# Moving a reduction to the end of VectorE's slot in a software-pipelined attention and FFN kernel

## The chip, the cores and the metric

The kernel runs on one core of a Trainium2 chip. The metric is the device time of one execution, in microseconds (us); the time before is the median of three executions. The core's engines are TensorE (PE in the profile), VectorE (DVE), ScalarE (ACT), GpSimd (POOL) and SyncE (SP), which here issues all DMAs. Each engine works through its own list of instructions in the order in which the program wrote them; the lists meet only at semaphores.

## The reference

For 4 sequences of 1024 rows and 256 channels, and a context of 154 rows of 192 channels for each, the reference computes cross attention and a gated FFN whose inputs and weights are rounded to blocks of 4-bit floats:

```
x  = x + attention(layernorm(x), ctx)       # 16 heads of 64, softmax over the 154 context rows, then Wo, bo
xq = fp4(layernorm(x))                      # blocks of 16: largest |x| / 6 is the scale, 8 magnitudes
h  = silu(xq @ fp4(w_gate).T) * (xq @ fp4(w_up).T)      # 704 wide
x  = x + fp4(h) @ fp4(w_down).T
```

## The kernel before

The 4096 rows are 32 tiles of 128 rows. `schedule` runs one **step** for each tile (`t = 2 * pair + par`), and each engine has its own function `step` with the same shape: a loop over 8 **slots** `k`. A slot is the unit of the software pipeline: in slot `k` of step `t` the kernel works on the pair of heads `u = k` (a *unit*) of tile `t`, and on later stages of older units and tiles: `e = t-1` (the end of its attention, then its layernorm and rounding), `f = t-2` (gate and up products, in quarters), `d = t-3` (the rounding of the hidden values and the down product), `c = t-4` (the output). The flags `own`, `before`, `gate`, `down` and `out_` say which of these exist. The first steps and one group of four steps in every eight also prepare keys, values and projected values of a sequence (`setup`, the jobs).

One unit passes through these stages:

- PE slot `k`: `scores` writes the scores of unit `k` into one of two PSUM banks `ps_s` (three matmuls, high and low parts of fp32 values). It waits for the exponentials of unit `k-2`, which free the bank.
- DVE slot `k`: the largest score of each of the two heads, negated, into `negmax` (L884).
- ACT slot `k`: two exponentials `probs <- ps_s` with `negmax` as the bias, which also make the sums (L678). They wait for `max_v`, the semaphore of L884.
- DVE slot `k+1`: `invert_sums` makes `rsum` (L848). POOL slot `k+1`: `normalise` multiplies the exponentials by it (L511).
- PE slot `k+2`: `turn_probs` transposes them into the one bank `ps_t` (L1213). It waits until the low parts of the unit before it are out of that bank.
- ACT slot `k+3`: `weights_hi` copies `ps_t` into `pT_hi` (L572), the first work of the slot. DVE slot `k+3`: `weights_lo` takes the difference, `pT_lo` (L737, a helper that makes all low parts).
- PE slot `k+4`: `attend` multiplies by the projected values.

In the kernel before DVE's slot `k` is in this order: `invert_sums` of unit `k-1`; the low parts of unit `k-3` (and in slot 2 those of `xqT`, in slots 5 and 6 those of `hqT`); **the largest score of unit `k`**; then everything else: the output sum in slot 0, the low part of a query product (`q_lo`), the jobs, `stats` in slot 4, `silu` and `hidden` of one FFN quarter in slots 3 to 6, block maxima and scales, the powers that round the values, and the residual sum `x1` in slot 3.

ACT's slot `k` is: `weights_hi` of unit `k-3`, other high parts, `tanh` of a quarter in slots 3 to 6, the exponentials of unit `k`, and behind them in slot 2 the copy `y <- x1` (L698), in slot 4 the next tile's layernorm (`layer_norm1_out`, L601), in slot 5 the layernorm of `x1` into `xn` (L689). DVE's slot 5 reads `xn` (`largest(xn, ...)`, L764); POOL's slot 6 multiplies it by `xri` (L552) behind `normalise` of unit 5, and DVE's slot 6 waits for that before `power(xn, ...)` (L784).

Of the kernel before, what the change touches and what calls it, by code (L numbers as in the profile page):

```python
# [5 lines left out]
ALU = mybir.AluOpType  # L6
ACT = mybir.ActivationFunctionType
AX_X = mybir.AxisListType.X
# [15 lines left out]
def xattn_ffn_kernel(nc: bass.Bass, x, ctx_768, Wq, Wk, Wv, Wo, bo, w_gate, w_up, w_down, out):  # L24
# [8 lines left out]
    PAIRS = H // 2  # L33
# [7 lines left out]
    UM = 2 * M  # L41
# [13 lines left out]
    with ExitStack() as stack:  # L55
        def sb(name, shape, dt=F32):
            return stack.enter_context(nc.sbuf_tensor(name, shape, dt))

        def sem(name):
            return stack.enter_context(nc.semaphore(name))  # L60
# [29 lines left out]
        negmax = sb("negmax", [P, H])  # L90
# [5 lines left out]
        st2, mv2, rs2, nm2 = ln[1]  # L96
# [3 lines left out]
        x1 = [x1_both[:, i, :] for i in range(2)]  # L100
        y_xn = sb("y_xn", [P, 3 * C])
        y, xn = [y_xn[:, i * C:(i + 1) * C] for i in range(2)], y_xn[:, 2 * C:3 * C]
# [29 lines left out]
        def bank(name):  # L132
            return stack.enter_context(nc.psum_tensor(name, [P, 512], F32))

        ps_t, ps_q, ps_o, ps_m = (bank(n) for n in ("ps_t", "ps_q", "ps_o", "ps_m"))
        ps_s = [bank("ps_s0"), bank("ps_s1")]
# [26 lines left out]
        s_mm, max_v, exp_a, rsum_v, norm_p = (sem(n) for n in ("s_mm", "max_v", "exp_a", "rsum_v", "norm_p"))  # L163
        t_mm, pT_hi, pT_lo, o_mm = sem("t_mm"), sem("pT_hi"), sem("pT_lo"), sem("o_mm")
        xr_p, x1_v, ln2_v, ln2_p, xln2_a = (sem(n) for n in ("xr_p", "x1_v", "ln2_v", "ln2_p", "xln2_a"))
        xq_v, xq_p, xqT_mm, xqT_hi, xqT_lo = (sem(n) for n in ("xq_v", "xq_p", "xqT_mm", "xqT_hi", "xqT_lo"))
# [9 lines left out]
        def some(count):  # L176

            return not isinstance(count, int) or count > 0
# [28 lines left out]
        def q_slots(t, par):  # L207
            return {k: k + 2 for k in range(PAIRS - 2)} if isinstance(t, int) and t == 0 else Q_SLOTS[par]

        def q_unit(t, par, k):  # L210
            return q_slots(t, par).get(k)
# [24 lines left out]
        def jobs_at(setup, k):  # L236
            return JOBS[setup[0]].get(k, []) if setup else []

        def jobs_before(setup, k):

            if not setup or k > 0:
                return jobs_at(setup, k - 1)
            kind, b = setup
            if kind == "roll":
                return JOBS["k"][SLOTS - 1]
            if kind == "settle":
                return JOBS["start" if b == 0 else "roll"].get(SLOTS - 1, [])
            return []
# [320 lines left out]
        def _(act):  # L569
            def hi_part(dst, src, ready, done):  # L570
                act.wait_ge(*ready)
                act.activation(dst, src, ACT.Copy).then_inc(done, 1)  # L572
# [72 lines left out]
            def step(pair, par, own=True, before=True, gate=True, down=True, out_=True, ahead=True, queries=True,  # L645
                     setup=None):
                t = 2 * pair + par
                e, f, d = t - 1, t - 2, t - 3
                for k in range(SLOTS):
                    if before and k < 3:  # L650
                        weights_hi(e, k + PAIRS - 3)
                    if own and k >= 3:
                        weights_hi(t, k - 3)
                    if gate and k == 2:
                        hi_part(xqT[0][:, :, :], parts(ps_m, KT), (xqT_mm, f + 1), xqT_hi)
                    if down and k in (5, 6):
                        r = k - 5
                        hi_part(hqT[0][:, 3 * r:3 * r + 3, :], parts(ps_m, 3), (hqT_mm, 2 * d + r + 1), hqT_hi)
                    if own and ahead and par == 0 and k == 7:
                        hi_part(xT_all(0), parts(xT_bank(setup), 4), (xT_mm, pair + 2), xT_hi)  # L660
                    if own and queries and q_unit(t, par, k - 1) is not None:
                        q_hi_part(pair + par, q_unit(t, par, k - 1))
                    for job in jobs_before(setup, k):
                        take_hi(job, setup[1])
                    if gate and 3 <= k < Q + 3:
                        q = k - 3
                        quarter = slice(q * QF, (q + 1) * QF)
                        if q == 0 and not some(f):
                            act.wait_ge(raw_mm, RAW_T[DOWN])
                        elif q == 0:  # L670
                            act.wait_ge(hq_v, 9 * f - 2)
                        act.wait_ge(gu_mm, Q * f + q + 1)
                        act.activation(eh[:, quarter], ps_g[q % 2][:, 0:QF], ACT.Tanh, scale=0.5).then_inc(th_a, 1)
                    if own:
                        act.wait_ge(max_v, PAIRS * t + k + 1)
                        for s in range(2):
                            h = 2 * k + s
                            ins = act.activation(probs[:, h, 0:M], ps_s[k % 2][:, s * M:(s + 1) * M], ACT.Exp,  # L678
                                                 bias=negmax[:, h:h + 1], accum_out=sums[:, h:h + 1])
                        ins.then_inc(exp_a, 1)  # L680
                    if isinstance(t, int) and t == 0 and k == 1:
                        layer_norm1_out(2, 0)
                    if own and ahead and k == 4:
                        layer_norm1_out(t + 3, 1 - par)
                    if before and k == 5:
                        act.wait_ge(ln2_p, 4 * e + 4)
                        if some(e):
                            act.wait_ge(xqT_mm, e)
                        act.activation(xn, x1[1 - par], ACT.Identity, bias=nm2[:, :], scale=rs2[:, :])\  # L689
                           .then_inc(xln2_a, 1)  # L690
                    if turn_at(t, k, 0) is not None:
                        chunk_hi(turn_at(t, k, 0))
                    if down and k == 2:
                        at = pair - 2 + par
                        act.wait_ge(x1_v, d + 1)
                        if some(at):
                            act.wait_ge(st_y[1 - par], 16 * at)
                        act.activation(y[1 - par], x1[1 - par], ACT.Copy).then_inc(y_a, 1)  # L698
# [34 lines left out]
        def _(dve):  # L733
# [5 lines left out]
            def q_lo_part(pair, u):  # L739
                lo_part(q_sb[1][:, u, :], ps_q[:, 0:2 * P], q_sb[0][:, u, :], (q_hi, PAIRS * pair + u + 1), q_lo)  # L740
# [26 lines left out]
            def fp4_scales(am, sc, ri, v, before):  # L767

                dve.wait_ge(v, before + 1)
                dve.tensor_scalar(sc, am, 1.0 / 6.0, LEAST_SCALE, ALU.mult, ALU.max).then_inc(v, 1)  # L770
                dve.wait_ge(v, before + 2)
                dve.reciprocal(ri, sc).then_inc(v, 1)
# [23 lines left out]
            for half in range(2):  # L796
                h = slice(D - D * half, P - D * half)
# [48 lines left out]
            def invert_sums(t, u):  # L846
                dve.wait_ge(exp_a, PAIRS * t + u + 1)
                dve.reciprocal(rsum[:, 2 * u:2 * u + 2], sums[:, 2 * u:2 * u + 2]).then_inc(rsum_v, 1)  # L848
# [14 lines left out]
            def step(pair, par, own=True, before=True, gate=True, down=True, out_=True, ahead=True, queries=True,  # L863
                     setup=None):
                t = 2 * pair + par
                e, f, d, c = t - 1, t - 2, t - 3, t - 4
                for k in range(SLOTS):
                    if before and k == 0:
                        invert_sums(e, PAIRS - 1)
                    if own and k >= 1:  # L870
                        invert_sums(t, k - 1)
                    if before and k < 3:
                        weights_lo(e, k + PAIRS - 3)
                    if own and k >= 3:
# [3 lines left out]
                    if down and k in (5, 6):  # L878
                        r = k - 5
                        lo_part(hqT[1][:, 3 * r:3 * r + 3, :], parts(ps_m, 3), hqT[0][:, 3 * r:3 * r + 3, :],  # L880
                                (hqT_hi, 2 * d + r + 1), hqT_lo)
                    if own:
                        dve.wait_ge(s_mm, PAIRS * t + k + 1)
                        dve.tensor_reduce(negmax[:, 2 * k:2 * k + 2],  # L884
                                          ps_s[k % 2][:, 0:UM].rearrange("p (h m) -> p h m", h=2),
                                          AX_X, ALU.max, negate=True).then_inc(max_v, 1)
                    if out_ and k == 0:
                        dve.wait_ge(d_mm, c + 1)
                        dve.wait_ge(y_a, c + 1)
# [2 lines left out]
                        lo_part(xT_all(1), parts(xT_bank(setup), 4), xT_all(0), (xT_hi, pair + 2), xT_lo)  # L892
                    if own and queries and q_unit(t, par, k - 1) is not None:
                        q_lo_part(pair + par, q_unit(t, par, k - 1))
                    for job in jobs_before(setup, k):
                        take_lo(job, setup[1])
                    if turn_at(t, k, 1) is not None:
# [53 lines left out]
                    if gate and k == 7:  # L951
                        if some(f):
                            dve.wait_ge(hq_p, 3 * f)
                        fp4_scales(hri[:, :], hsc[:, :], hri[:, :], hq_v, 9 * f + 3)

            def gate_by_up(n, q, eh_, bank_):
                quarter = slice(q * QF, (q + 1) * QF)
# [450 lines left out]
```

## Time and profile before

| what | value |
|---|---|
| median of 3 executions | 902.29 us (901.35 to 903.94) |
| the profiled execution: its time | 904.46 us |
| its span, first to last instruction | 902.3 us |
| PE, DVE, ACT, POOL busy | 842.0, 710.2, 523.1, 539.2 us |
| mean granted TensorE clock | 0.987 |
| a step of the steady part (two in turn) | 23.70 and 23.32 us |

Busy is the time in which an engine had an instruction in work. Records on one engine overlap a little: a record lasts some hundredths of a microsecond into the next one, and overlapped time is counted once. The chain of work that ended last is 68% PE and 20% DVE.

### The profile page before, as it was taken

What the parts mean: (1) busy time and instruction counts of PE and PEld (TensorE: products, weight loads), DVE (VectorE), ACT (ScalarE), POOL (GpSimd) and SP (SyncE); (2) the same over time, 40 slices, a digit from 0 to 9 for tenths busy, and PEclk for the clock granted to TensorE, in tenths of its full rate; (3) what the DMA queues carried; (4) which work ended last, traced back from release to release, by engine and by line L of the source; (5) the groups of instructions that cost most, each with busy time, mean ns of one, the idle gap of its engine ahead of it and who ended that gap; (6) DMA issues with size and microseconds to landing.
All of it is one profiled execution on the core that took longest, in us unless ns stands there. A gap on an engine that the chain in (4) does not pass through costs nothing.

```text
span 902.3 us, 19161 instructions
## 1 busy us (share of the span) xinstructions
PE 842.0 (93%) x6278; PEld 807.9 (90%) x6278; DVE 710.2 (79%) x2157; ACT 523.1 (58%) x1878; POOL 539.2 (60%) x810
## 2 busy tenths in 40 slices
PE   4887899999999999999999999999999999999986
PEld 4766789999988999999988999999988999999876
DVE  5659788877777888887877888886877888887787
ACT  4554466665665565657655665666665665665531
POOL 6438776765644666665553666665644566666643
PEclk9889999999999999999999999999999999999999
DMA  8101000001010000001010000000100000000000
GB/s 243 38 23 44 7 19 7 24 14 47 8 36 19 13 25 13 25 13 42 13 35 21 13 18 14 24 14 12 49 7 19 12 15 23 14 18 14 7 7 18
DMA packets 20137, 23.14 MB, mean 26 GB/s; under 512 B 2658, under 2 KB 18250, under 8 KB 20042
## 3 DMA queue, kind: packets, MB, share of 16 engines
q1 hardware_dynamic: 20042, 21.94, 8.0%
q8 instruction: 52, 0.85, 0.4%
q14 instruction: 43, 0.35, 0.1%
HBM read 17.74 MB, written 4.19 MB: 24 GB/s over the span
## 4 chain that ended last, share of the span: by engine, by line
PE 68%; DVE 20%; issue 4%; ACT 4%; POOL 2%; DMA 1%; SPq 0%; DVEq 0%; ACTq 0%
PE ps_q L1161 10%; PE ps_g L1246 9%; PE ps_s L1203 9%; PE ps_t L1213 6%; PE ps_o L1226 5%; PE ps_o L1228 5%; PE ps_o L1227 5%; PE ps_g L1124 3%; DVE pT_lo L737 3%; DVE scales L764 3%; DVE negmax L884 3%; PE ps_m L1260 2%; PE ps_m L1262 2%; PE ps_m L1261 2%; PE ps_m L1089 2%
## 5 line engine op out<-in xcount | busy, mean ns | idle before, releaser
L511 POOL TENSOR_TENSOR probs<-probs,rsum 128x308 f32<-128x308 f32 x256 | 179.7, 702 | 260.6 <-DVE rsum L848 260.1
L678 ACT ACTIVATE probs<-ps_s,negmax 128x154 f32<-128x154 f32 x512 | 194.8, 386 | 217.7 <-DVE negmax L884 216.5
L884 DVE TENSOR_REDUCE negmax<-ps_s 128x2 f32<-128x308 f32 x256 | 121.0, 473 | 90.7 <-PE ps_s L1203 89.9
L1226 PE MATMUL ps_o<-B_sb,pT_lo 128*128 128x256 f32 x640 | 180.9, 283 | 0.9 <-DVE x_both L939 0.6
L1228 PE MATMUL ps_o<-B_sb,pT_hi 128*128 128x256 f32 x640 | 180.7, 282 | 0.0
L1227 PE MATMUL ps_o<-B_sb,pT_hi 128*128 128x256 f32 x640 | 180.4, 282 | 0.0
L737 DVE TENSOR_TENSOR pT_lo<-ps_t,pT_hi 128x256 fp32r<-128x256 f32 (+1 forms) x256 | 122.8, 480 | 34.4 <-ACT pT_hi L572 34.0
L1213 PE MATMUL ps_t<-ident,probs 128*128 128x128 f32 x640 | 113.6, 276 | 25.0 <-DVE pT_lo L737 21.9
L1246 PE MATMUL ps_g<-WGU,xqT_hi 128*128 128x352 f32 x504 | 131.8, 343 | 2.0 <-DVE B_sb L737 1.7
L1226 PEld LDWEIGHTS ps_o<-B_sb,pT_lo 128*128 128x128 f32 x640 | 121.0, 189 | 1.4 <-issue 0.8
L1228 PEld LDWEIGHTS ps_o<-B_sb,pT_hi 128*128 128x128 f32 x640 | 121.4, 190 | 0.0
L1227 PEld LDWEIGHTS ps_o<-B_sb,pT_hi 128*128 128x128 f32 x640 | 121.2, 189 | 0.0
L572 ACT ACTIVATE pT_hi<-ps_t 128x256 fp32r<-128x256 f32 (+1 forms) x256 | 111.2, 434 | 5.6 <-PE ps_t L1213 3.4
L1213 PEld LDWEIGHTS ps_t<-ident,probs 128*128 128x128 f32 x640 | 73.6, 140 | 37.2 <-issue 33.9
L678 ACT ACTIVATION_READ_ACCUMULATOR probs<-ps_s,negmax 128x1 f32 x512 | 100.9, 197 | 0.0
L1203 PE MATMUL ps_s<-K_hi,q_lo 128*128 128x308 f32 x256 | 86.8, 339 | 0.0
L1161 PE MATMUL ps_q<-xT_hi,Wq_lo 128*128 128x256 f32 x256 | 79.9, 312 | 7.2 <-DVE q_lo L737 4.4
L1246 PEld LDWEIGHTS ps_g<-WGU,xqT_hi 128*128 128x128 f32 x504 | 82.1, 189 | 3.0 <-DVE B_sb L737 2.4
L1246 PE MATMUL ps_g<-WGU,xqT_lo 128*128 128x352 f32 x252 | 81.1, 322 | 0.0
L1203 PE MATMUL ps_s<-K_hi,q_hi 128*128 128x308 f32 x256 | 78.1, 305 | 0.0
L1203 PE MATMUL ps_s<-K_lo,q_hi 128*128 128x308 f32 x256 | 77.8, 304 | 0.0
L475 POOL TENSOR_TENSOR hn<-hn,hc 128x704 f32<-128x704 f32 x31 | 52.8, 1704 | 39.1 <-DVE hc L789 39.1
(228 smaller groups left out, 2218.3 us busy)
## 6 DMA issues: line engine op xcount, KB each, us to landing
xa<-in_x_dram SPq DMA_DIRECT2D x33, 128.0 KB, 2.1
xr<-in_x_dram SPq DMA_DIRECT2D x32, 128.0 KB, 2.0
out_dram<-y_xn SPq DMA_DIRECT2D x30, 128.0 KB, 1.7
W_sb<-in_L_xattn_Wk_dram SPq DMA_DIRECT2D x4, 512.0 KB, 3.7
W_sb<-in_L_xattn_Wv_dram SPq DMA_DIRECT2D x3, 512.0 KB, 3.3
probs<-in_L_xattn_Wq_dram SPq DMA_DIRECT2D x2, 512.0 KB, 8.6
Wo_sb<-in_L_xattn_Wo_dram SPq DMA_DIRECT2D x1, 1024.0 KB, 9.7
VT<-in_L_ffn_w_down_dram SPq DMA_DIRECT2D x2, 352.0 KB, 3.8
```

Of the source, the lines that this page charges most:

```text
L511: pool.tensor_tensor(unit, unit, rsum[:, 2 * u:2 * u + 2].unsqueeze(2) .to_broadcast([P, 2, M]), ALU.mult).then_inc(norm_p, 1)
L572: act.activation(dst, src, ACT.Copy).then_inc(done, 1)
L678: ins = act.activation(probs[:, h, 0:M], ps_s[k % 2][:, s * M:(s + 1) * M], ACT.Exp, bias=negmax[:, h:h + 1], accum_out=sums[:, h:h + 1])
L737: dve.tensor_tensor(dst, src, hi.bitcast(F32), ALU.subtract).then_inc(done, 1)
L884: dve.tensor_reduce(negmax[:, 2 * k:2 * k + 2], ps_s[k % 2][:, 0:UM].rearrange("p (h m) -> p h m", h=2), AX_X, ALU.max, negate=True).then_ ...
L1161: ins = pe.matmul(ps_q[:, 0:2 * P], Wq_sb[w][:, k, u * P:(u + 1) * P], xT[x_][:, k, :], start=(i == 0), stop=(i == len(terms) - 1))
L1203: ins = pe.matmul(ps_s[u % 2][:, 0:UM], q_sb[a][:, u, par * P:(par + 1) * P], K_sb[b][:, u, :], start=(i == 0), stop=(i == len(terms) - 1))
L1213: ins = pe.transpose(ps_t[:, j * P:(j + 1) * P], probs_rows[:, at:at + P], ident[:, :])
L1226: pe.matmul(ps_o[:, 0:C], lo[:, j, :], w[:, 0:C], start=first, stop=False)
L1227: pe.matmul(ps_o[:, 0:C], hi[:, j, :], w[:, C:2 * C], start=False, stop=False)
L1228: ins = pe.matmul(ps_o[:, 0:C], hi[:, j, :], w[:, 0:C], start=False, stop=last)
L1246: ins = pe.matmul(ps[:, 0:2 * QF], x_[:, k, :], WGU[:, k, a, :, q * QF:(q + 1) * QF], start=(i == 0), stop=(i == len(terms) - 1))
```

## The change

On DVE the largest score of unit `k` goes from the middle of slot `k` to its very end. `invert_sums` goes from the front of the slot to behind `q_lo`. On ACT the layernorm of `x1` into `xn` goes from behind the exponentials of slot 5 to ahead of them. No instruction is added or removed; no buffer, tile, semaphore count or DMA is changed.

```diff
@@ ACT, step
+                    if before and k == 5:
+                        act.wait_ge(ln2_p, 4 * e + 4)
+                        if some(e):
+                            act.wait_ge(xqT_mm, e)
+                        act.activation(xn, x1[1 - par], ACT.Identity, bias=nm2[:, :], scale=rs2[:, :])\
+                           .then_inc(xln2_a, 1)
                     if own:
                         act.wait_ge(max_v, PAIRS * t + k + 1)
                         for s in range(2):
...
-                    if before and k == 5:
-                        act.wait_ge(ln2_p, 4 * e + 4)
-                        if some(e):
-                            act.wait_ge(xqT_mm, e)
-                        act.activation(xn, x1[1 - par], ACT.Identity, bias=nm2[:, :], scale=rs2[:, :])\
-                           .then_inc(xln2_a, 1)
@@ DVE, step
                 for k in range(SLOTS):
-                    if before and k == 0:
-                        invert_sums(e, PAIRS - 1)
-                    if own and k >= 1:
-                        invert_sums(t, k - 1)
                     if before and k < 3:
                         weights_lo(e, k + PAIRS - 3)
                     if own and k >= 3:
                         weights_lo(t, k - 3)
...
-                    if own:
-                        dve.wait_ge(s_mm, PAIRS * t + k + 1)
-                        dve.tensor_reduce(negmax[:, 2 * k:2 * k + 2],
-                                          ps_s[k % 2][:, 0:UM].rearrange("p (h m) -> p h m", h=2),
-                                          AX_X, ALU.max, negate=True).then_inc(max_v, 1)
...
                     if own and queries and q_unit(t, par, k - 1) is not None:
                         q_lo_part(pair + par, q_unit(t, par, k - 1))
+                    if before and k == 0:
+                        invert_sums(e, PAIRS - 1)
+                    if own and k >= 1:
+                        invert_sums(t, k - 1)
...
                         fp4_scales(hri[:, :], hsc[:, :], hri[:, :], hq_v, 9 * f + 3)
+                    if own:
+                        dve.wait_ge(s_mm, PAIRS * t + k + 1)
+                        dve.tensor_reduce(negmax[:, 2 * k:2 * k + 2],
+                                          ps_s[k % 2][:, 0:UM].rearrange("p (h m) -> p h m", h=2),
+                                          AX_X, ALU.max, negate=True).then_inc(max_v, 1)
```

## Rows read from the trace of the kernel before

**Rows 1.** The page's first part: busy us, share of the span, instructions.

```profile
PE 842.0 (93%) x6278; PEld 807.9 (90%) x6278; DVE 710.2 (79%) x2157; ACT 523.1 (58%) x1878; POOL 539.2 (60%) x810
```

**Rows 2.** Waits of the whole execution: us in total, times, longest us.

```profile
ACT probs L678 <- DVE negmax L884: 216.5, 228, 2.8
DVE negmax L884 <- PE ps_s L1203: 89.9, 101, 5.7
...
DVE pT_lo L737 <- ACT pT_hi L572: 34.0, 95, 3.8
...
PE ps_t L1213 <- DVE pT_lo L737: 21.9, 37, 2.9
...
DVE scales L764 <- ACT y_xn L689: 17.3, 28, 1.1
```

**Rows 3.** Timeline of DVE across the end of one slot and the next.

```profile
513.01 0.47 DVE L884 TENSOR_REDUCE negmax<-ps_s 128x2 f32<-128x308 f32 x1
513.40 0.41 DVE L737 TENSOR_TENSOR q_lo<-ps_q,q_hi 128x256 fp32r<-128x256 f32 x1
513.73 0.33 DVE L764 TENSOR_REDUCE scales<-eh 128x11 f32<-128x176 f32 x1
514.16 0.19 DVE L770 TENSOR_SCALAR scales<-scales 128x44 f32<-128x44 f32 x1
...
514.73 0.11 DVE L848 RECIPROCAL rsum<-sums 128x2 f32<-128x2 f32 x1
514.78 0.56 DVE L737 TENSOR_TENSOR pT_lo<-ps_t,pT_hi 128x384 fp32r<-128x384 f32 x1
```

**Rows 4.** Timeline of ACT: the same slot, then slot 2's and slot 4's extra work.

```profile
513.51 0.39 ACT L678 ACTIVATE probs<-ps_s,negmax 128x154 f32<-128x154 f32 x1 [0.77 <-DVE negmax L884]
...
514.26 0.49 ACT L572 ACTIVATE pT_hi<-ps_t 128x384 fp32r<-128x384 f32 x1
...
522.74 0.41 ACT L698 ACTIVATE y_xn<-x_both 128x256 f32<-128x256 f32 x1
523.04 0.38 ACT L572 ACTIVATE pT_hi<-ps_t 128x256 fp32r<-128x256 f32 x1
...
528.28 0.59 ACT L601 ACTIVATE xa<-xa,small 128x256 f32<-128x256 f32 x1
528.77 0.38 ACT L572 ACTIVATE pT_hi<-ps_t 128x256 fp32r<-128x256 f32 x1
```

**Rows 5.** Two consecutive steady steps by windows, same columns as in rows 6.

```profile
516.37:540.07 23.70, 23.27 (x184) 22.92 (x183) 20.28 (x64) 14.81 (x55) 15.52 (x25) 1.00 0.07 23
540.07:563.39 23.32, 22.80 (x180) 22.44 (x179) 18.99 (x63) 13.88 (x54) 15.53 (x25) 1.00 0.05 13
```

**Rows 6.** Windows, first to last L884: us; PE, PEld, DVE, ACT, POOL busy; clock.

```profile
24.20:98.63 74.43, 58.58 (x367) 50.85 (x366) 55.59 (x140) 37.84 (x123) 42.81 (x57) 0.91 0.11 32
98.63:194.37 95.74, 90.44 (x698) 88.19 (x699) 76.74 (x247) 56.89 (x217) 65.41 (x98) 1.00 0.05 15
194.37:402.39 208.02, 203.37 (x1554) 196.75 (x1553) 166.56 (x519) 127.74 (x462) 124.47 (x193) 1.00 0.07 22
...
818.41:860.83 42.42, 40.17 (x308) 39.01 (x306) 34.19 (x109) 25.02 (x97) 25.85 (x37) 1.00 0.03 10
```

**Rows 7.** Timeline of POOL in one slot 6.

```profile
510.09 0.70 POOL L511 TENSOR_TENSOR probs<-probs,rsum 128x308 f32<-128x308 f32 x1 [3.07 <-DVE rsum L848]
510.75 0.62 POOL L552 TENSOR_TENSOR y_xn<-y_xn,scales 128x256 f32<-128x256 f32 x1
```

**Rows 8.** Timeline of DVE in the same slot 6.

```profile
509.85 0.15 DVE L848 RECIPROCAL rsum<-sums 128x2 f32<-128x2 f32 x1
...
511.23 0.33 DVE L854 SCALAR_TENSOR_TENSOR gu<-eh,ps_g 128x176 f32<-128x176 f32 x1
...
512.09 0.28 DVE L784 TENSOR_SCALAR hc<-y_xn 128x256 uint32<-128x256 uint32 x1
```

**Rows 9.** Windows of 5 us in the first 125 us, columns as in rows 6.

```profile
85.00:90.00 5.00, 2.38 (x19) 1.99 (x17) 3.75 (x11) 2.02 (x8) 4.76 (x7) 1.00 0.00 0
90.00:95.00 5.00, 3.77 (x21) 3.80 (x22) 4.72 (x14) 2.11 (x8) 4.04 (x6) 0.72 0.00 0
95.00:100.00 5.00, 3.67 (x29) 3.50 (x28) 4.49 (x9) 2.37 (x11) 4.31 (x5) 0.94 0.00 0
...
120.00:125.00 5.00, 3.71 (x31) 3.52 (x30) 4.90 (x14) 2.73 (x12) 3.95 (x6) 1.00 0.19 52
```

## The prediction

> **What bounds the kernel now.** I read the page's busy times first. PE is busy in 93% of the span and DVE in 79% [rows 1], so an order of work that makes DVE wait has some 20% of the span to spend before it shows, and no more. Next come the waits [rows 2]: PE hardly waits (its longest entry is the wait for `pT_lo`, 21.9 us in 37 times), DVE waits 89.9 us for the scores before it takes a largest score, and ACT waits 216.5 us for that. Two entries matter for the change: DVE waits 34.0 us for `pT_hi`, in 95 of 256 slots, and 17.3 us for `xn`.
>
> Then I follow one slot on two engines. DVE ends the largest score of unit 7 at 513.01 + 0.47 = 513.48 [rows 3]. ACT starts the exponentials 0.03 later, at 513.51, and can begin the slot's `pT_hi` only behind them, at 514.26; it ends at 514.75 [rows 4]. DVE starts the `pT_lo` that needs it at 514.78 [rows 3]. From the end of the largest score to the start of `pT_lo` are 1.30 us, and DVE is not idle in them: it makes `q_lo`, block maxima and scales, and inverts sums [rows 3]. So the order before has a loop through both engines (largest score, exponentials, `pT_hi`, `pT_lo`, next largest score), and DVE's other work lies in the part of the loop that is ACT's. The 34.0 us of waits for `pT_hi` are the slots in which that work was a little too short.
>
> A steady step of 8 slots takes 23.70 or 23.32 us; PE is busy in 23.27 and 22.80 of them, DVE in 20.28 and 18.99 [rows 5]. So PE sets the time, and DVE has 3.4 and 4.3 us a step left, about 0.48 us a slot.
>
> **The change part by part.**
>
> *The largest score last.* Whatever DVE does in a slot now stands ahead of L884, and the first thing of the next slot is `weights_lo`, which waits for `pT_hi`. On ACT `weights_hi` of the next slot is queued behind this slot's exponentials, and these wait for L884. Nothing is left on DVE between the two: it must stand still for the whole ACT part of the loop, in every slot. Its price goes by rows 3 and 4: 0.03 hand-over to ACT; 514.26 - 513.51 = 0.75 from the start of the exponentials to the start of `pT_hi`; `pT_hi` itself, 0.49 for three blocks and 0.38 for two, which alternate, so 0.435; 0.03 hand-over back. Together 1.245 us a slot. ACT's work behind the exponentials is in the same gap: the copy of `y` in slot 2 (523.04 - 522.74 = 0.30, in 29 steps), the next layernorm in slot 4 (528.77 - 528.28 = 0.49, in 30 steps) [rows 4], and early on 10 copies of weight chunks, which I take at 0.5 each, near a `pT_hi` of three blocks.
>
> That is what the loop costs DVE. What it saves is no more than DVE's present waits: 89.9 us for scores that will now be there long before, and the 34.0 us, which become part of the new gap. They are not subtracted below, since I build the new time from DVE's busy time alone.
>
> PE hides none of it. Its `turn_probs` waits for the low part of the unit before, because `ps_t` is one bank, so PE is tied to the loop once a slot. It needs about 23.3 us a step [rows 5] and will get more than 31; scores, gate products and query products for a slot are then finished before DVE asks for them. SP's loads and stores are issued behind waits for `x1`, `y` and PE's transposes and only get more time; the moved pieces issue no DMA.
>
> *`invert_sums` behind the low parts.* It no longer stands ahead of `weights_lo`, and the exponentials it waits for are done by then, as `pT_hi` is queued behind them. It costs nothing on DVE. POOL's `normalise` starts later, and PE needs it only in its next slot, over 2 us on. If that cover were gone, PE would wait up to the 0.70 of L511 [rows 7] a slot. One place has no cover: in slot 6 POOL makes `normalise` of unit 5 and behind it the product of `xn`, and DVE's `power` waits for the product. POOL's product ends 510.75 + 0.62 - 509.85 = 1.52 us after the start of `rsum` [rows 7, 8]. Behind `rsum` DVE will have only `silu`, `hidden` and one block maximum ahead of `power`: 512.09 - 511.23 = 0.86, and 0.08 for `rsum` itself [rows 8]; before, a `pT_lo`, a `hqT_lo` and a largest score were there too. That leaves a new wait of 0.58 us a step, 18 us over 31 steps.
>
> *`xn` ahead of slot 5's exponentials.* L884 of slot 5 now stands behind `largest(xn)`, so the exponentials can't be ahead of `xn`. ACT makes it while it waits for L884 anyway, and DVE's 17.3 us of waits [rows 2] go. By the sum below, which holds no such waits, it costs and gives nothing more. Bounds: 0, and 0.5 us a step if ACT got to it late.
>
> *The sum.* Between the first and the last largest score, at 24.20 and 860.83, DVE is busy 55.59 + 76.74 + 3 x 166.56 + 34.19 = 666.2 us [rows 6] (the stretch of 208 us occurs three times, with the same busy time). To that come gaps between DVE's own dependent instructions, such as 514.16 - (513.73 + 0.33) = 0.10 [rows 3]; idle time that has no releaser adds up to 21.5 us over the 32 steps. Then 255 gaps of 1.245 (317.5), ACT's extra work (8.7 + 14.7 + 5 = 28.4) and slot 6 (18). That makes 1051.6 us in place of 836.6. With 24.2 us ahead of it and 902.3 - 860.8 = 41.5 behind it, both unchanged, the span is 1117.
>
> Two places need more. In the first stretch DVE is idle for 74.43 - 55.59 = 18.8 us [rows 6], for transfers, PE at a lower clock and jobs; I guess that 8 us of it stay beside the new gaps. In the three steps in which a sequence's projected values are made PE has over 34 us of work, so that single slots will be PE's; 2 us each. With these 14 the span is 1131. The profiled execution's time lies 2.2 above its span and 2.2 above the median of the three, so 1131 is also the forecast of the median: 229 us or 25% slower. For a steady step the same rows give 20.28 + 0.7 + 8 x 1.245 + 0.8 + 0.6 = 32.3 and 31.0 us for the two kinds.
>
> *The clock.* PE would be busy for 23.3 of about 31.7 us, in pieces with idle gaps up to some 2 us in slots 5 and 6. A stretch in which PE was busy 3.71 of 5 us kept the granted clock of 1.00; after one with 2.38 of 5 the clock was 0.72 and then 0.94 [rows 9], between its levels of 2.4 and 1.2 GHz. That one drop took 5 x 0.28 + 5 x 0.06 = 1.7 us of PE's time. I take no loss, since most of PE's gaps are nearer to the first row; the bound is one drop a step that nothing absorbs, 32 x 1.7 = 54 us. The Trainium skill has a rule that speaks against the change here ("TensorE: Matmul & The Clock Gate", "A second HAM failure mode: psum-queue depth-cycling"): a TensorE that pauses briefly again and again between groups of matmuls lets its clock swing between both levels, and throughput goes down. By that rule the sum would be 1185 rather than 1131; this trace agrees for the one drop and not for the stretch with 3.71.
>
> **The rivals.**
>
> *PE's clock falls in most steps.* The mechanism is the last one. For it: the pauses in slots 5 and 6 come next to each other. Against it: a lower clock lengthens PE's work into idle time that it has plenty of. 1150 to 1240 us, 1185 with one drop a step.
>
> *POOL becomes the bound.* `rsum` comes later, and POOL carries the long hidden-value rounding in slots 1 to 3. If `turn_probs` then waited for L511 by about 1 us in three slots of 31 steps, the time would be 1131 + 93 = 1224. Against it: POOL is busy 15.5 us a step [rows 5], half of what a step will have.
>
> *Not slower.* If DVE's stop at L884 is what delays the low parts, moving it to the end sets them free: PE's waits for `pT_lo` (21.9 us) [rows 2] would go, which gives about 880. For it: DVE does wait 89.9 us at L884 for scores, with work behind it that could run. It decides if DVE's gap between L884 and the next `pT_lo` stays under the 0.48 us a slot that DVE has to spare. Rows 3 and 4 put it at 1.25 to 1.30, and no reordering on ACT shortens it.
>
> **How the numbers follow.** The forecast gets 0.80, the clock 0.12, POOL 0.04, "not slower" 0.04. Bounds below: no leftover waits (-14), no wait in slot 6 (-18), and 0.08 us less for each of 255 largest scores, by which records overlap their followers (-20): 1079. Above: leftover waits of 30 rather than 14, or one drop of the clock a step: 1147 to 1185, and 1190 with a little of both. The range is 1080 to 1190. A change within 0.3% is about what a measurement of this kernel can't tell from none: faster 0.03, same 0.01, slower 0.96.
>
> **What would show it.** DVE's waits for `pT_hi` would grow from 34.0 to about 300 us, in some 250 slots; its waits for scores and for `xn` would nearly vanish; PE's waits for `pT_lo` would grow from 21.9 to 200 us or more; a steady step would take 31 to 32 us with DVE busy as long as now. The prediction is wrong if `pT_lo` starts less than 1.2 us after the end of L884, or if PE is still busy in over 85% of a step with its clock at 1.00.

## The result, and the profile after

The change made the kernel slower by 27%: 1142.76 us (1141.63 to 1144.24, 4 runs) against 903.02 us, a ratio of 1.267 (95% interval 1.264 to 1.269). The forecast was 1131 with a range of 1080 to 1190.

The first part of the changed kernel's page, as [rows 1]:

```profile
PE 897.4 (79%) x6278; PEld 835.4 (73%) x6278; DVE 722.6 (63%) x2157; ACT 505.5 (44%) x1878; POOL 568.8 (50%) x810
...
DVE 50%; ACT 24%; issue 12%; PE 9%; POOL 5%; DVEq 0%; ACTq 0%; POOLq 0%
```

No engine fills the span any more; PE, the busiest, has gone from 93% to 79%. The second line is the chain of work that ended last: it was 68% PE, and is now half DVE and a quarter ACT. A chain that alternates between two engines while neither fills the span points to a loop of hand-overs; the runs below test that. The waits, as [rows 2] (us in total, times, longest):

```profile
ACT probs L684 <- DVE negmax L952: 583.6, 256, 4.5
...
DVE pT_lo L737 <- ACT pT_hi L572: 345.3, 256, 3.0
...
PE ps_t L1213 <- DVE pT_lo L737: 207.3, 166, 3.8
DVE hc L784 <- POOL y_xn L552: 15.9, 28, 0.8
```

ACT waits for the largest score in all 256 slots, and DVE waits for `pT_hi` in all 256: each of the two engines works while the other stands. The 89.9 us of waits for scores and the 17.3 us for `xn` are no longer among them; a wait of GpSimd's making in slot 6 is new. DVE's timeline over two slots, answering to [rows 3], and ACT's, answering to [rows 4]:

```profile
660.19 0.47 DVE L952 TENSOR_REDUCE negmax<-ps_s 128x2 f32<-128x308 f32 x1
662.34 0.42 DVE L737 TENSOR_TENSOR pT_lo<-ps_t,pT_hi 128x256 fp32r<-128x256 f32 x1 [1.68 <-ACT pT_hi L572]
...
665.48 0.47 DVE L952 TENSOR_REDUCE negmax<-ps_s 128x2 f32<-128x308 f32 x1
667.25 0.56 DVE L737 TENSOR_TENSOR pT_lo<-ps_t,pT_hi 128x384 fp32r<-128x384 f32 x1 [1.30 <-ACT pT_hi L572]
```

```profile
660.69 0.39 ACT L684 ACTIVATE probs<-ps_s,negmax 128x154 f32<-128x154 f32 x1 [2.26 <-DVE negmax L952]
...
661.44 0.59 ACT L601 ACTIVATE xa<-xa,small 128x256 f32<-128x256 f32 x1
661.93 0.38 ACT L572 ACTIVATE pT_hi<-ps_t 128x256 fp32r<-128x256 f32 x1
```

DVE has no row between 660.66 and 662.34, nor between 665.95 and 667.25. The first gap is longer because the next tile's layernorm lies in it. Two steady steps, as [rows 5], and the whole stretch from the first to the last largest score, as [rows 6]:

```profile
646.52:678.79 32.27, 25.00 (x177) 23.68 (x177) 20.23 (x65) 14.16 (x55) 16.74 (x25) 0.95 0.06 17
678.79:710.89 32.10, 25.56 (x181) 24.19 (x180) 19.62 (x63) 13.68 (x54) 16.72 (x25) 0.95 0.03 9
```

```profile
25.93:1097.87 1071.94, 854.18 (x6027) 795.34 (x6026) 678.30 (x2045) 485.33 (x1823) 537.88 (x767) 0.96 0.05 16
```

DVE is busy in a step about as long as before (20.23 and 19.62 us); the step is 8.6 and 8.8 us longer.

### The profile page after: what moved, and what is told of

The parts are those of the page before. It is cut to its first block, busy times and chain, and to the rows that moved or that the text cites. A ratio compares the mean times of both kernels' runs of the same rounds, so it can differ in the third digit from the quotient of the medians.

```text
span 1139.5 us, 19161 instructions
## 1 busy us (share of the span) xinstructions
PE 897.4 (79%) x6278; PEld 835.4 (73%) x6278; DVE 722.6 (63%) x2157; ACT 505.5 (44%) x1878; POOL 568.8 (50%) x810
## 4 chain that ended last, share of the span: by engine, by line
DVE 50%; ACT 24%; issue 12%; PE 9%; POOL 5%; DVEq 0%; ACTq 0%; POOLq 0%
ACT probs L684 12%; DVE negmax L952 8%; DVE pT_lo L737 7%; ACT pT_hi L572 7%; DVE q_lo L737 3%; DVE scales L764 3%; DVE hc L784 3%; DVE hqT_lo L737 2%; DVE gu L854 2%; DVE hn L778 2%; DVE hc L789 2%; DVE B_sb L737 2%; POOL probs L511 2%; DVE small L758 2%; DVE scales L772 2%
## 5 line engine op out<-in xcount | busy, mean ns | idle before, releaser
L511 POOL TENSOR_TENSOR probs<-probs,rsum 128x308 f32<-128x308 f32 x256 | 198.3, 775 | 517.8 <-DVE rsum L848 517.6
L737 DVE TENSOR_TENSOR pT_lo<-ps_t,pT_hi 128x256 fp32r<-128x256 f32 (+1 forms) x256 | 125.8, 491 | 345.3 <-ACT pT_hi L572 345.3
L1213 PE MATMUL ps_t<-ident,probs 128*128 128x128 f32 x640 | 119.6, 286 | 208.8 <-DVE pT_lo L737 207.3
L1213 PEld LDWEIGHTS ps_t<-ident,probs 128*128 128x128 f32 x640 | 68.4, 142 | 243.7 <-issue 241.5
L1226 PE MATMUL ps_o<-B_sb,pT_lo 128*128 128x256 f32 x640 | 184.3, 288 | 0.8 <-DVE x_both L934 0.5
L1227 PE MATMUL ps_o<-B_sb,pT_hi 128*128 128x256 f32 x640 | 183.8, 287 | 0.0
L1228 PE MATMUL ps_o<-B_sb,pT_hi 128*128 128x256 f32 x640 | 183.0, 286 | 0.0
L1226 PEld LDWEIGHTS ps_o<-B_sb,pT_lo 128*128 128x128 f32 x640 | 125.1, 195 | 1.2 <-issue 0.7
L1228 PEld LDWEIGHTS ps_o<-B_sb,pT_hi 128*128 128x128 f32 x640 | 124.9, 195 | 0.0
L1227 PEld LDWEIGHTS ps_o<-B_sb,pT_hi 128*128 128x128 f32 x640 | 124.9, 195 | 0.0
L952 DVE TENSOR_REDUCE negmax<-ps_s 128x2 f32<-128x308 f32 x256 | 117.7, 460 | 0.1
L1161 PE MATMUL ps_q<-xT_hi,Wq_hi 128*128 128x256 f32 x256 | 73.7, 288 | 0.0
```

What stands on the lines that cost most here:

```text
L511: pool.tensor_tensor(unit, unit, rsum[:, 2 * u:2 * u + 2].unsqueeze(2) .to_broadcast([P, 2, M]), ALU.mult).then_inc(norm_p, 1)
L737: dve.tensor_tensor(dst, src, hi.bitcast(F32), ALU.subtract).then_inc(done, 1)
L952: dve.tensor_reduce(negmax[:, 2 * k:2 * k + 2], ps_s[k % 2][:, 0:UM].rearrange("p (h m) -> p h m", h=2), AX_X, ALU.max, negate=True).then_ ...
L1161: ins = pe.matmul(ps_q[:, 0:2 * P], Wq_sb[w][:, k, u * P:(u + 1) * P], xT[x_][:, k, :], start=(i == 0), stop=(i == len(terms) - 1))
L1213: ins = pe.transpose(ps_t[:, j * P:(j + 1) * P], probs_rows[:, at:at + P], ident[:, :])
L1226: pe.matmul(ps_o[:, 0:C], lo[:, j, :], w[:, 0:C], start=first, stop=False)
```

## The experiments

Each ratio is to the kernel before, run beside it.

**The largest score alone.** The changed kernel with `invert_sums` back in front.

```diff
 after.py, DVE
+                    if before and k == 0:
+                        invert_sums(e, PAIRS - 1)
+                    if own and k >= 1:
+                        invert_sums(t, k - 1)
                     if before and k < 3:
                         weights_lo(e, k + PAIRS - 3)
...
-                    (the same four lines behind q_lo)
```

> The changed kernel with the sums taken back to the front of DVE's slot; only the largest score stays last (and the normalised x1 ahead of slot 5's exponentials, which it needs). Theory A (a loop largest score, exponentials, pT_hi, pT_lo with nothing of DVE's in the gap): still about 345 us of DVE waits for pT_hi; only slot 6's wait for GpSimd (15.8 us) goes, so 1127 us, 1120 to 1135. Rival B (the late sums make GpSimd, and so TensorE's transposes, late): most of the loss is given back, 900 to 950 us.

Measured: 1101.37 us, ratio 1.220 (1.217 to 1.223). This is far from rival B and below theory A's interval. The loop stays: most of the loss comes from the largest score's place. But 41 us go, not 16. The waits show where DVE's gap has its parts now:

```profile
DVE rsum L848 <- ACT probs L684: 235.1, 256, 0.9
...
DVE pT_lo L737 <- ACT pT_hi L572: 63.9, 190, 1.6
```

`rsum` waits for the exponentials, runs inside the gap, and `pT_lo` waits for the rest. The wait for GpSimd is gone. So the late sums cost more than the forecast gave them.

**The sums alone**, in the kernel before: the four lines go from the front of the slot to behind `q_lo`.

> The kernel before with the sums alone moved behind the low parts. Theory A: no more than noise to +0.8%, 900 to 910 us; DVE's waits for exponentials (6.7 us) go, a wait for GpSimd in slot 6 of up to 0.6 us a step comes and lies in DVE's spare time. Rival B: over 1000 us.

Measured: 933.07 us, ratio 1.033 (1.030 to 1.036). Neither expectation: the sums are no rival for the loss, but they are not free. DVE waits 15.6 us for GpSimd's `xn` in slot 6, 28 times, and PE's waits for `pT_lo` grow from 21.9 to 42.2 us.

**`xn` alone**, in the kernel before: ACT's six lines go ahead of the exponentials of slot 5.

> The kernel before with only ScalarE's piece moved: x1's normalised values ahead of slot 5's exponentials. Theory A: DVE's 17.3 us of waits for them go, and with them TensorE's 0.5 us wait for pT_lo in every second step: 893 to 902 us. Rival C (the exponentials of slot 5 come later by 0.5 us and are on the path): 905 to 918 us.

Measured: 887.70 us, ratio 0.983 (0.980 to 0.985). This is 1.7% faster than the kernel before, and more than theory A gave it (893 to 902). A pair of steady steps, as [rows 5]:

```profile
506.81:529.97 23.16, 23.09 (x184) 22.91 (x183) 20.18 (x63) 14.81 (x55) 15.56 (x25) 1.00 0.08 23
529.97:552.43 22.46, 22.46 (x180) 22.46 (x179) 18.90 (x62) 14.11 (x54) 15.54 (x25) 1.00 0.05 14
```

PE is busy in all of the second and in all but 0.07 us of the first. DVE's 17.3 us of waits for `xn` are gone, and the time is 14.7 us shorter; PE's waits for `pT_lo` fell from 21.9 to 13.0. That the waits for `xn` lay in slots in which DVE had nothing to spare is the likely reason why so much of them reached the end; it was not traced slot by slot.

**`pT_hi` ahead of the exponentials**, in the changed kernel.

```diff
 after.py, ACT
-                    if before and k < 3:
-                        weights_hi(e, k + PAIRS - 3)
-                    if own and k >= 3:
-                        weights_hi(t, k - 3)
...
+                    if before and k < 2:
+                        weights_hi(e, k + PAIRS - 2)
+                    if own and k >= 2:
+                        weights_hi(t, k - 2)
                     if own:
                         act.wait_ge(max_v, PAIRS * t + k + 1)
...
-                for u in range(PAIRS - 3, PAIRS):
+                for u in range(PAIRS - 2, PAIRS):
                     weights_hi(T, u)
```

> The changed kernel, but ScalarE makes a slot's pT_hi ahead of the exponentials of the slot before, so that pT_lo no longer waits for them. Theory A: the waits for pT_hi (345 us) nearly vanish, and smaller ones take their place, for the high parts and tanh that are still behind the exponentials, some 0.8 us a slot after pT_lo has run: about 6.6 us a step instead of 10.8, so about 1010 us, 985 to 1040. Rival D (TensorE's clock or GpSimd sets the changed kernel's time): within 3% of 1143 us.

Measured: 1021.32 us, ratio 1.132 (1.129 to 1.135), as the loop has it. The waits moved to what is still behind the exponentials:

```profile
DVE q_lo L737 <- ACT q_hi L572: 81.8, 86, 2.2
...
DVE hqT_lo L737 <- ACT hqT_hi L572: 65.4, 58, 1.5
```

**A dose on ACT**, in the changed kernel and in the one before, behind the exponentials (the copies compute nothing that is used):

```diff
                         ins.then_inc(exp_a, 1)
+                        act.wait_ge(ident_p, 2)
+                        for s in range(2):
+                            at = F + 8 * k + 4 * s
+                            act.activation(eh[:, at:at + 4], ident[:, 0:4], ACT.Copy)
```

> The changed kernel with two tiny ScalarE copies (128x4, into unused columns) behind each slot's exponentials, ahead of the next pT_hi; they compute nothing that is used. Theory A: they lie on the loop, so each adds its start-to-start time 256 times: with 0.1 to 0.2 us each, 1195 to 1245 us, and the waits of DVE for pT_hi grow by the whole of it. Rival D (TensorE's clock or GpSimd sets the time): under 1160 us.

> The same two tiny copies in the kernel before. Theory A: DVE has work to do while ScalarE is busy with them, so that most slots hide them; only the slots that waited for pT_hi already pay: 902 to 925 us, at most a third of what the changed kernel pays. Rival (ScalarE's work costs the same in both kernels): 955 to 1005 us.

Measured: 1187.97 us with the change (ratio 1.317, 1.315 to 1.319) and 913.32 us without (1.012, 1.010 to 1.015). In the changed kernel ACT's timeline shows what the copies take:

```profile
660.88 0.30 ACT L690 ACTIVATE eh<-ident 128x4 f32<-128x4 f32 x2
661.08 0.49 ACT L572 ACTIVATE pT_hi<-ps_t 128x384 fp32r<-128x384 f32 x1
```

The pair moves `pT_hi` by 0.18 to 0.20 us; times 256 that is 46 to 51, and the kernel paid 1187.97 - 1142.76 = 45.2. DVE's waits for `pT_hi` grew by 392.1 - 345.3 = 46.8. The copies were a little cheaper than I had put them, so the time fell below the interval that theory A named; but nearly all of what they took reached the end. In the kernel before the same copies cost 11.5 us, a quarter: there ACT's time behind the exponentials is mostly covered by DVE's work, and DVE's waits for `pT_hi` grew by 14.8 us only (34.0 to 48.8).

**Two places between.** The kernel with sums in front and `xn` ahead, with L884's lines behind `q_lo`, or behind `hidden`.

> Sums in front, x1's normalised values ahead of slot 5's exponentials, and the largest score in a third place: behind the query's low part, ahead of all FFN work. Theory A: what DVE still has behind it covers the 1.245 us of ScalarE in most slots; open are about 0.8 in slot 1, 0.9 in slot 2, 0.3 in 3 and in 7, 2.5 us a step, so that DVE's step is as long as TensorE's 23.3: 884 to 905 us. Rival E (any move of the largest score behind other work costs its own length on the path): over 930 us.

> The same, with the largest score behind silu and hidden, ahead of the rounding work. Theory A: open are 0.8 in slot 1, 1.55 in slot 2, 0.9 in slot 3, 1.5 in slot 4, 0.4 in slots 6 and 7 each, together 5.5 us a step in place of the 10.8 of the version with the largest score last: about 951 us, 930 to 975. Rival D: as the version with the largest score last, 1101.

Measured: 888.47 us (ratio 0.985, 0.983 to 0.986) and 944.60 us (1.046, 1.044 to 1.048). With the first place and with the last one these make a series in which only the work behind the largest score changes:

| largest score stands | us |
|---|---|
| ahead of `q_lo` (`xn` alone) | 887.70 |
| behind `q_lo`, ahead of the FFN work | 888.47 |
| behind `silu` and `hidden` | 944.60 |
| last | 1101.37 |

The first move costs nothing, though it makes the exponentials later in the slots that have a `q_lo`. Some slots are short of cover there, and DVE's waits for ACT show it: those for `pT_hi`, for `rsum`'s exponentials and for `q_hi` add up to 83.8 us against 44.8 with `xn` alone. But DVE's waits for scores fell from 90.4 to 37.9:

```profile
DVE negmax L892 <- PE ps_s L1203: 37.9, 40, 3.6
```

So the shortfall came out of time in which DVE stood for PE anyway. The loss begins when the shortfalls against ACT's 1.25 us, added up over a step, make DVE's step longer than PE's. Added up slot by slot they gave 884 to 905 us for the first middle place, where 888.47 was measured, and about 951 for the second, where it was 944.60.

**Where the sums' cost lies.** Two more versions of the sums alone: `invert_sums` in front in slot 6, or in slots 0 and 6.

```diff
 before.py with the sums moved, DVE
+                    if own and k == 6:
+                        invert_sums(t, k - 1)
                     if before and k < 3:
...
-                    if own and k >= 1:
+                    if own and k >= 1 and k != 6:
                         invert_sums(t, k - 1)
```

> The kernel before with the sums moved behind the low parts in every slot but 6, where they stay in front. Theory F (the 30 us that the sums cost alone are mainly DVE's new wait for GpSimd in slot 6, 0.61 us a step, which falls where DVE has no time to spare): two thirds of the loss go, 908 to 916 us. Rival G (the loss is GpSimd's normalise running into DVE's rounding instructions in slots 0 and 7, which then take 0.84 in place of 0.53 us): 925 to 933 us, hardly better.

> The same with the sums left in front in slots 0 and 6. Theory F: as with slot 6 alone, within 3 us of it. Rival G: a further 8 us or more less than that, as the rounding instruction of slot 0 takes 0.53 us again.

Measured: 912.66 us (1.011, 1.009 to 1.012) and 912.77 us (1.011, 1.009 to 1.013). Slot 6 holds 20 of the 31 us, as theory F has it. The second run tells nothing on slot 0: the rounding instruction there still took 0.78 us on average rather than 0.54, so the collision was not taken away. What the last 11 us are stays open.

**`xn` ahead and `pT_hi` early**, in the kernel before.

> The kernel before with x1's normalised values ahead of slot 5's exponentials and, besides, ScalarE's pT_hi a slot earlier, ahead of the exponentials. Theory A: DVE's remaining waits for pT_hi (34 us) go, and with them most of TensorE's remaining 13 us of waits for pT_lo: 872 to 886 us. Rival: ScalarE now waits for TensorE's transposes ahead of the exponentials and makes these late: 888 to 900 us.

Measured: 900.20 us, ratio 0.998 (0.997 to 0.999): a miss for theory A, at the upper end of its rival's interval, and 12.5 us worse than `xn` alone. ACT now waits 279.7 us for PE's transposes, in 253 slots, and the exponentials behind them are late: DVE's waits for them ahead of `rsum` grow from 6.8 (with `xn` alone) to 76.3 us. Taking one wait out of the loop by tying ACT to PE made another.

**The sums in front in slots 0 and 6**, in the changed kernel.

> The changed kernel with the sums back in front in slots 0 and 6 alone. Theory H (the 41 us between the changed kernel and the one with all sums in front are three things: 15.8 us of waits for GpSimd in slot 6, some 7 us by which DVE's rounding instruction of slot 0 and GpSimd's normalise run into each other, and the rest because the sums in front lie in DVE's gap and behind it do not): 16 and 7 us go and two eighths of the rest, 1112 to 1120 us, with the wait for GpSimd near 0 and L784 at 0.53 us again. Rival I (all of it is the place of the sums in the gap): 1130 to 1136 us, a quarter of the 41.

Measured: 1118.97 us, ratio 1.241 (1.237 to 1.244). This lies in theory H's interval, but one of its terms did not come. DVE's wait for GpSimd in slot 6 fell from 15.9 to 0.8 us. The rounding instruction of slot 0 (L784) takes 0.54 us again, but the one ahead of it (L778) is longer. Busy time in us and mean ns, in the changed kernel and then in this one:

```profile
L778 DVE SCALAR_TENSOR_TENSOR hn<-eh,scales 128x704 f32<-128x704 f32 x31 | 27.8, 898 | 0.0
L784 DVE TENSOR_SCALAR hc<-hn 128x704 uint32<-128x704 uint32 x31 | 23.5, 757 | 3.1
```

```profile
L778 DVE SCALAR_TENSOR_TENSOR hn<-eh,scales 128x704 f32<-128x704 f32 x31 | 37.7, 1215 | 0.0
L784 DVE TENSOR_SCALAR hc<-hn 128x704 uint32<-128x704 uint32 x31 | 16.7, 538 | 3.1
```

L784 gave back 6.8 us and L778 took 9.9: the collision with GpSimd moved from one to the other.

## Why the prediction was right, and which steps were off

*The largest score last* was right, in mechanism and in size. The gap was worked out as 1.245 us in each slot and 28 us of ACT's other work, 345.9 us in all; DVE's waits for `pT_hi` measured 345.3 us in 256 slots. In slots without other ACT work `pT_lo` starts 1.30 us behind the end of the largest score (now L952) where a unit has three blocks and 1.19 where it has two; the mean is the forecast's, though 1.19 is a hundredth under the 1.2 that was named as a sign of being wrong:

```profile
648.18 0.42 DVE L737 TENSOR_TENSOR pT_lo<-ps_t,pT_hi 128x256 fp32r<-128x256 f32 x1 [1.19 <-ACT pT_hi L572]
```

The other sign did not come: PE is busy in 77 and 80% of a step. Three kinds of run show that these waits are the loop and not a by-product: taking `pT_hi` out of it gave 121 us back, other waits taking the rest of its place; adding to it cost 45 us for the 46 to 51 added; and leaving work behind the largest score hid it.

*The sum* came to a span of 1131 where 1139.5 was measured. Its terms against the trace, between the first and the last largest score: DVE busy 666.2 forecast, 678.3 measured; waits for `pT_hi` 345.9 and 344.6; slot 6 18 and 15.9; gaps of DVE's own 21.5 and 21.1; leftover waits 14 and 12.0. Ahead of it 24.2 and 25.9, behind it 41.5 and 41.6. The miss is DVE's busy time, +12.1. The term took it as unchanged. The largest part of the miss is the largest score itself: in the kernel before, the next instruction starts 0.39 us after L884 does (513.01 to 513.40 [rows 3]), inside its record of 0.47, and overlapped time counts once; now nothing starts until the whole record is over (660.19 + 0.47, then the gap). Over all slots that is 17.3 us more. The forecast knew of this overlap, but only as 20 us less, in its lower bound: it has the wrong sign there. `hc <- hn` (L784) grew by 6.9 us for the reason in the last section, `rsum` counts 7.1 less because more of it is overlapped, and the rest are small terms of either sign. Of the two steady steps the first came out as forecast (32.3, measured 32.27), the second did not (31.0, measured 32.10). DVE is busy 0.6 us longer in it than the forecast had and idle 0.4 longer; the cause stays open.

*`invert_sums` behind the low parts* was the step that failed, in part. "It costs nothing on DVE" holds neither in the changed kernel, where the move costs 41 us, nor in the kernel before, where it costs 31. The forecast had only the wait in slot 6 (18 us, measured 15.9). It overlooked that in front `rsum` would lie in DVE's new gap, ahead of `pT_lo`, and be free there, while behind `q_lo` it adds its 0.07 us from start to start in every slot (256 x 0.07 = 18 us). With the largest score alone the waits of the gap are 299.0 us against 346.2, and `rsum` counts 29.9 us more from its start to the next one's: 17 net, added up over DVE's rows. The forecast also overlooked the collision with GpSimd, but in the changed kernel that is little of the 41: with the sums in front L784 takes 6.8 us less and L778 5.6 more (33.4 against 27.8). Some 7 of the 41 us stay open. The sum was hardly hurt, because it was built from DVE's whole busy time, `rsum` included. The sums are what the prediction mis-sized as an edit, not as a term.

*`xn` ahead* was right for the changed kernel: its waits vanish. The prediction didn't ask what it would bring without the rest: 14.7 us.

*The clock.* The fall that was feared came, and cost nearly nothing. The granted clock in 5 us windows of the changed kernel, columns as in [rows 9]:

```profile
665.00:670.00 5.00, 3.03 (x25) 2.85 (x25) 3.02 (x11) 1.82 (x7) 1.28 (x2) 1.00 0.00 1
670.00:675.00 5.00, 2.71 (x20) 2.54 (x19) 3.45 (x10) 1.70 (x7) 1.58 (x3) 0.90 0.17 52
675.00:680.00 5.00, 5.00 (x34) 5.00 (x33) 2.97 (x6) 1.86 (x9) 3.42 (x4) 0.76 0.10 30
```

Behind the pauses of slots 5 and 6 PE goes from 2.4 GHz towards 1.2 GHz, and from 680 to 685 us it has 1.00 again; both steady steps above have a mean of 0.95. Of 32 us that is 1.6, as much as the one drop in [rows 9] took: the bound's one drop a step. But PE's work only gets longer into its own idle time: DVE waits 0.1 us for scores, ACT 4.1 us for the transposes ahead of `pT_hi`, and DVE's waits for the down product (`y`, L881) are 3.4 us, in the whole execution. The Trainium skill's rule that a TensorE with many short pauses swings between its clocks ("TensorE: Matmul & The Clock Gate", "A second HAM failure mode: psum-queue depth-cycling") agrees with these windows; the loss of throughput that it goes with was not on the path here.

*The rivals.* GpSimd did not become the bound: PE's waits for L511 are 0.5 us. "Not slower" fails at the point that was named for it, a gap under 0.48 us a slot. That "no reordering on ACT shortens it" was too strong: `pT_hi` ahead of the exponentials is such a reordering, and 121 us came back.

## What to carry to other kernels

When engines hand work to each other in a fixed order, ask of each wait what the waiting engine has behind it and what the awaited engine has ahead of it: a producer's last instruction in its slot must not feed the consumer's first work that the producer's next slot needs. A short reduction belongs where the producer still has as much work behind it as the consumer takes to answer; here that was about 1.25 us, and a slot with less cover cost nothing as long as the producer had time in its step to spare. When parts of a change move in opposite directions, time each alone: the piece that was only there to keep the order legal was worth 1.7% by itself, and that version (887.70 us) beats both kernels.

## What the runs showed of the hardware

GpSimd and VectorE got into each other's way in slot 0, where the late sums put `normalise` beside VectorE's rounding. VectorE, then GpSimd, in the changed kernel:

```profile
644.78 0.87 DVE L778 SCALAR_TENSOR_TENSOR hn<-eh,scales 128x704 f32<-128x704 f32 x1
645.76 0.84 DVE L784 TENSOR_SCALAR hc<-hn 128x704 uint32<-128x704 uint32 x1
```

```profile
644.95 1.27 POOL L511 TENSOR_TENSOR probs<-probs,rsum 128x308 f32<-128x308 f32 x1 [1.03 <-DVE rsum L848]
```

`normalise` takes 0.70 us alone [rows 7] and 1.27 here: it begins inside L778 and ends 0.57 us behind L778's end at 645.65. L784, which takes 0.54 when GpSimd is clear of it, begins while `normalise` runs and ends 0.38 us behind its end at 646.22. In both cases the later of the two lost most of what it overlapped with the earlier: 0.57 of 0.70 us, and 0.30 of 0.46. With the sums in front in slots 0 and 6 another pair meets, GpSimd's next product first:

```profile
403.49 0.73 POOL L532 TENSOR_TENSOR xr<-xr,bo_all 128x256 f32<-128x256 f32 x1
```

```profile
403.60 1.36 DVE L778 SCALAR_TENSOR_TENSOR hn<-eh,scales 128x704 f32<-128x704 f32 x1
```

L778, which takes 0.88 us clear of GpSimd, loses 0.48 of the 0.62 us that it overlaps. The Trainium skill has a rule for such pairs ("SBUF — State Buffer", "Who interferes with whom"): VectorE and GpSimd share a pair of ports that one instruction holds until it ends, when VectorE's instruction has two SBUF inputs or runs in a two-port mode. These rows agree with it but for 0.13 to 0.16 us of each overlap that the later instruction did not lose. L778 has two SBUF inputs (`eh` and `scales`), L784 one; the modes themselves no run here shows.
